# Handing the norm's reciprocal roots to all partitions through DRAM instead of TensorE, with every queue reordered

## What is computed

```python
q = softmax(Wq @ layernorm(x), over the 64 rows of a head) * SCALE
k = softmax(Wk @ ctx, over positions);  v = Wv @ ctx
out = Wo @ (per head: (k v^T)^T q) + bo                  # 128 x 1024 per batch
norm = max(sqrt(sum(out * out over the 128 channels)), 1e-12)
x = x + tanh(g_xattn) * out / norm * g * sqrt(128)
gate, up = bitlinear(layernorm(x), w_gate), bitlinear(layernorm(x), w_up)   # 2752 wide
x = x + tanh(g_ffn) * bitlinear(gate * up, w_down)
```

## Time and profile before

| | us |
|---|---|
| median of 3 runs (lowest, highest) | 1388.72 (1384.52, 1388.87) |
| span of the profiled execution, first to last instruction | 1386.2 |
| PE busy in it | 1314.9 (95%) |
| DVE busy | 1003.7 (72%) |
| ACT busy | 634.1 (46%) |
| POOL busy | 580.5 (42%) |

### The profile page before, as it was taken

One profiled execution on the slowest core, in us unless ns is written; L12 is line 12 of the kernel. 1 busy time (PEld: TensorE's weight loads), 2 busy tenths in 40 slices (PEclk: granted clock), 3 DMA queues, 4 the chain that ended last, 5 costly groups with the idle time before them and its releaser, 6 DMA issues. The chain is left out here.

```text
span 1386.2 us, 30208 instructions
## 1 busy us (share of the span) xinstructions
PE 1314.9 (95%) x12408; PEld 961.9 (69%) x12408; DVE 1003.7 (72%) x1343; ACT 634.1 (46%) x879; POOL 580.5 (42%) x357
## 2 busy tenths in 40 slices
PE   4787599999999899999999999999999999999999
PEld 2454387855787558876598757885598748985994
DVE  6977778878799976887688875889578866641330
ACT  4668786853544424453434533453344443320220
POOL 0249925866274472444334451346034432240120
PEclk8998799999999999999999999999999999999999
DMA  9939999896664879778777975787677895663421
GB/s 352 408 145 336 267 288 306 243 184 151 146 163 99 174 180 244 182 181 186 168 176 174 196 187 136 200 169 186 150 184 181 179 171 130 159 173 88 138 76 46
DMA packets 401417, 260.00 MB, mean 188 GB/s; under 512 B 325312, under 2 KB 342080, under 8 KB 401280
## 3 DMA queue, kind: packets, MB, share of 16 engines
q1 hardware_dynamic: 394368, 232.90, 67.3%
q10 hardware_dynamic: 6912, 25.17, 5.7%
HBM read 152.37 MB, written 25.95 MB: 129 GB/s over the span
## 5 line engine op out<-in xcount | busy, mean ns | idle before, releaser
L1118 PE MATMUL ps<-w_dn,inter_buf 128*128 128x512 fp8e4 x1376 | 307.8, 380 | 2.0 <-DVE inter_buf L1372 1.3
L1118 PEld LDWEIGHTS ps<-w_dn,inter_buf 128*128 128x128 f16 x1376 | 134.9, 99 | 157.8 <-issue 4.7
L1804 POOL TENSOR_TENSOR qs<-qs,q_stat 128x1024 f32<-128x1024 f32 x64 | 129.6, 2024 | 232.9 <-DVE q_stat L1615 232.9
L1034 PE MATMUL ps<-zT,w_gu 128*128 128x256 f16 x1664 | 191.2, 274 | 3.0 <-DVE zT L1372 2.4
L1034 PEld LDWEIGHTS ps<-zT,w_gu 128*128 128x128 fp8e4 x1664 | 163.0, 99 | 29.2 <-DVE zT L1372 2.6
L1069 PE MATMUL ps<-w_gu 128*128 128x128 f16 x2880 | 174.0, 219 | 2.7 <-DVE w_gu L1715 1.8
L1069 PEld LDWEIGHTS ps<-w_gu 128*128 128x128 fp8e4 x2880 | 165.8, 98 | 7.1 <-issue 3.1
L1860 POOL TENSOR_TENSOR w_gu<-w_gu 128x512 f32<-128x512 f32 x60 | 82.4, 1373 | 179.8 <-DVE w_gu L1715 112.6
L1069 PE MATMUL ps<-zT,w_gu 128*128 128x128 f16 x2176 | 132.6, 219 | 0.0
L1715 DVE SCALAR_TENSOR_TENSOR w_gu<-ps,w_gu 128x512 f32<-128x512 f32 x120 | 82.5, 688 | 68.0 <-PE ps L1069 67.9
L1069 PEld LDWEIGHTS ps<-zT,w_gu 128*128 128x128 fp8e4 x2176 | 125.5, 98 | 3.9
(11 more groups left out here) (195 smaller groups left out, 2588.8 us busy)
## 6 DMA issues: line engine op xcount, KB each, us to landing
w_gu<-forms SPq DMA_DIRECT2D x158, 256.0 KB, 3.0
ct_raw<-forms SPq DMA_DIRECT2D x52, 256.0 KB, 3.1
w_dn<-in_down_w SPq DMA_DIRECT2D x19, 512.0 KB, 6.0
xb<-in_x ACTq DMA_DIRECT2D x16, 512.0 KB, 6.8
x_dram<-xb SPq DMA_DIRECT2D x16, 512.0 KB, 3.9
fin<-x_dram SPq DMA_DIRECT2D x32, 256.0 KB, 2.9
out<-fin SPq DMA_DIRECT2D x32, 256.0 KB, 2.4
inter_buf<-in_up_w SPq DMA_DIRECT2D x15, 512.0 KB, 9.7
```

Source lines behind the costliest of these rows:

```text
L1034: last = nc.tensor.matmul(ps[:, rest_bank(g, j), s * T:s * T + T], w_gu[:, w, k, :], zT[:, h, k, :], start=(k == 0 and h == 0), stop=(k == ...
L1118: mm = nc.tensor.matmul(ps[:, down_bank(g, k), :], inter_of(g, j, u % 2, b), w_dn[:, j, hf * 512:hf * 512 + 512], start=(u == 0), stop=(u ...
L1804: nc.gpsimd.tensor_tensor(v, v, q_stat[:, u % 2, 1, :].unsqueeze(2).broadcast_to([P, 2 * HEADS, DH]), ALU.mult).then_inc(q_prob, 1)
```

## The change

`R` goes. SP gets two steps instead: `put_r` stores the 128 by 4 values of `rsv` to 2 KB of DRAM as 512 pieces of 4 bytes, and `get_r` loads these 2 KB back once for each of the 128 partitions, into `sq`, whose square is no longer needed by then. `x2m` reads `sq` and waits for that load. Bank OUT is free for the next `outp` after `ssg`, no longer after `x2m`. `rs` waits for the store of two halves earlier, since `rsv` has two buffers. All numbers of `WHEN` are new (of the table a line or two is shown).

```diff
     "rs": (2, 0, B), 
-    "R": (2, 0, B),
+    "put_r": (2, 0, B), "get_r": (2, 0, B),
...
+    "put_r": [164, 248, 349, 411, 673, 778, 935, 989, 1091, 1155, 1333, ...],
+    "get_r": [196, 303, 374, 421, 692, 794, 972, 991, 1125, 1163, 1353, ...],
...
+    r_dram = nc.dram_tensor("r_dram", [2 * B, 512], F32, kind="Internal").ap()
...
+            def put_r(i, hf):
+                wait(sp, rs_ready, 2 * i + hf + 1)
+                sp.dma_start(r_dram[2 * i + hf, :].rearrange("(k p) -> p k", p=P),
+                             rsv[:, hf, :], allow_slow_non_contiguous=True).then_inc(r_stored, 16)
+
+            def get_r(i, hf):
+                wait(sp, r_stored, 16 * (2 * i + hf + 1))
+                sp.dma_start(sq, r_dram[2 * i + hf:2 * i + hf + 1, :].broadcast_to([P, 512])).then_inc(r_in, 16)
...
-            def R(i, hf):
-                wait(pe, rs_ready, 2 * i + hf + 1)
-                wait_banks(out_free)
-                for k in range(4):
-                    last = nc.tensor.transpose(ps[:, OUT, k * P:k * P + P],
-                                               rsv[:, hf, k:k + 1].broadcast_to([P, P]), ident[:, :])
-                last.then_inc(r_ready, 1)
-                out_free[0] = (y_scaled, 2 * i + hf + 1)
...
             def x2m(i, hf):
-                wait(dve, r_ready, 2 * i + hf + 1)
+                wait(dve, r_in, 16 * (2 * i + hf + 1))
                 wait(dve, y_ready, 2 * i + hf + 1)
...
-                nc.vector.scalar_tensor_tensor(out=y, in0=ps[:, OUT, :], scalar=small[:, COEF_X:COEF_X + 1],
+                nc.vector.scalar_tensor_tensor(out=y, in0=sq, scalar=small[:, COEF_X:COEF_X + 1],
...
             def rs(i, hf):
                 wait(pool, ss_guarded, 2 * i + hf + 1)
-                wait(pool, r_ready, 2 * i + hf - 1)
+                wait(pool, r_stored, 16 * (2 * i + hf - 1))
```

More of the change, by code:

```diff
@@ L79 @@
     "e_f": (4, 0, BY_PE), "qf_hi": (4, BY_PE, B), "qf_lo": (4, BY_PE, B), "turn_q": (4, BY_PE, B),
-    "outp": (8, 0, B), "yev": (2, 0, B), "ss": (2, 0, B), "ssg": (2, 0, B), "rs": (2, 0, B), "R": (2, 0, B),
+    "outp": (8, 0, B), "yev": (2, 0, B), "ss": (2, 0, B), "ssg": (2, 0, B), "rs": (2, 0, B),
+    "put_r": (2, 0, B), "get_r": (2, 0, B),
     "ld_xr": (1, 0, B), "x2m": (2, 0, B), "x2a": (2, 0, B), "st_x2": (1, 0, B), "ln2": (1, 0, B),
@@ new lines @@
+    "outp": [175, 176, 177, 182, 250, 251, 252, 257, 322, 324, 325, 353, 390, 400, 401, 402, 637, 638, 639, 640,
[6 rows of a table added]
+    "yev": [190, 255, 368, 399, 669, 759, 924, 963, 1081, 1131, 1327, 1386, 1520, 1634, 1736, 1797, 1930, 1977,
[3 rows of a table added]
+    "ssg": [183, 274, 356, 410, 677, 777, 921, 971, 1079, 1158, 1345, 1396, 1543, 1636, 1761, 1824, 1954, 1992,
[3 rows of a table added]
+    "ld_xr": [0, 147, 592, 614, 1097, 1124, 1546, 1587, 1969, 1984, 2371, 2478, 2810, 2864, 3244, 3363],
[9 rows of a table added]
+    "zt_hi": [367, 464],
+    "zt_lo": [359, 475],
+    "z_hi": [865, 1038, 1378, 1456, 1806, 1863, 2057, 2301, 2671, 2727, 2908, 3170, 3452, 3507],
@@ new lines @@
+    "st_out": [978, 1008, 1088, 1417, 1471, 1472, 1522, 1660, 1859, 1915, 2022, 2026, 2332, 2333, 2524, 2577, 2739,
+        2756, 2886, 2887, 3189, 3190, 3234, 3333, 3521, 3536, 3570, 3603, 3700, 3706, 3713, 3715],
+    "lmax": [21, 22, 23],
+    "lsum": [47, 48, 54],
+    "lscale": [44, 45, 49],
+    "l_hi": [33, 43, 132],
+    "l_lo": [56, 206, 246],
+    "wpart": [211, 212, 671],
+    "wtotal": [225, 241, 661],
+    "wscale": [223, 228, 689],
+    "consts": [5],
+    "prod": [20],
+    "gains": [30],
@@ L331 @@
+    "get_r": [196, 303, 374, 421, 692, 794, 972, 991, 1125, 1163, 1353, 1425, 1577, 1640, 1773, 1821, 1958, 1990,
+        2163, 2262, 2372, 2427, 2607, 2666, 2807, 2836, 3075, 3103, 3221, 3297, 3421, 3481],
 }
@@ L800, in _ @@
                      "turn_k": turn_k, "turn_q": turn_q, "turn_z": turn_z, "turn_zs": turn_zs, "store_form": store_form,
-                     "load_form": load_form, "st_x2": st_x2, "reload": reload,
+                     "load_form": load_form, "put_r": put_r, "get_r": get_r, "st_x2": st_x2, "reload": reload,
                      "st_out": st_out})
@@ L1123, in _ @@
             program({"prod": prod, "lsum": lsum, "csum": csum, "msum": msum, "kt": kt, "qt": qt, "tr": tr,
-                     "mprod": mprod, "ctxk": ctxk, "ktr": ktr, "zt": zt, "wtotal": wtotal, "outp": outp, "ss": ss, "R": R,
+                     "mprod": mprod, "ctxk": ctxk, "ktr": ktr, "zt": zt, "wtotal": wtotal, "outp": outp, "ss": ss,
                      "gu": gu, "product": product, "down": down})
```

266 lines of the change are left out of this document (114 added, 152 removed), and 199 rows, old and new, of the table WHEN.

## The result

| kernel | runs | median us | lowest to highest |
|---|---|---|---|
| before | 4 | 1386.9 | 1384.5 to 1388.9 |
| changed | 4 | 1649.5 | 1641.8 to 1674.9 |

The ratio is 1.187 (95% interval 1.184 to 1.191): 263 us slower. Forecast were 1380, 1370 to 1393. The page of the changed kernel, span 1648.8 us: its first lines and slices, and the start of its last chain.

A forecast was written before the change was run, and what follows sets the result against it. TensorE was taken to bound the time behind 175 us, the chain to the first gu before it. Terms -12.3 - 1.3 + 3 + 2 = -8.6 gave a span of 1377.6, plus 2.5 around it: 1380 us, range 1370 to 1393.

The forecast's parts named there:

- What bounds the kernel now: Whole kernel: behind 175 us TensorE's work sets the time; ahead, the chain to the first gu at 173.1 us.
- The transposes removed: TensorE: 28 R of batches 2 to 15, 0.44 us each, save 12.3 us; the four in front count as nothing.
- Six matmuls moved: Front: batch 3's first kt goes ahead of the first gu, into a PE wait for zT, saving 1.3 us.
- The store and the load added: DMA trip of rsv through DRAM: store 2.9 us, load 2.9, bounds 2.0 each to 9.1 for a DMA.
- What the round trip is added to: Halves behind 175 us: values in SBUF 7.1 us behind ss; late x2m steps cost 3 us, bounds 0 and 7.
- The chain to the first gu: Front, batch 1: trip about even with slack, SP's later turn_k delays gu 2 us, bounds -2 and +12.
- The store of small pieces is slow: Rival, every trip: store lands X us later than forecast, making the kernel slower from X of about 4; chance 0.12.
- X = 6: Store landing 6 us later than forecast: 19 us lost behind 175 us, 10 in front, 1409 us in all.
- More than the transposes: Rival, whole kernel: no wait added, some old waits go, gu 2 us earlier; -16 as the middle, 1372 us; chance 0.13.
- The front pays it back: Rival, 140 to 175 us: small transfers behind weight loads make gu 10 us later, 1388 us; chance 0.18.

The follow-up runs named there:

- e_notrip: The changed kernel with neither store nor load, its order kept, x2m multiplying by the squares in the tile and waiting for rs alone; 1396.4 us.
- e_getonly: The changed kernel without the store, its load replaced by one of the same size from a row of x that waits for rs alone; 1391.9 us.
- e_quick16: The changed kernel storing 128 pieces of 16 bytes, with ScalarE writing the squares in turned order; 1418.0, 1418.6 and 1431.5 us, ratio 1.026.
- o_notrip: The kernel before, in its old order, without the transposes R and with nothing in their place; 1383.6 us, ratio 0.997.

## Why the prediction was wrong

*"What bounds the kernel now"* was right: two regimes, and in the second a wait of PE is paid in full. It left out the clock: with PE idle for 211 us behind 175 us, in many short waits, the mean granted clock there was 0.93 instead of 1.00, and with 128 matmuls fewer in the whole kernel PE was busy 60 us longer.

*"The transposes removed"*: 12.3 us, measured 4 (2 to 6 by the interval). PE's busy time behind 175 us fell by 10.3, not 12.3, and 4.3 us came back as idle time, nearly all of it in the one wait for nothing that shows. The four in front were worth nothing, as said.

*The new order* had no price in the sum but for the six matmuls. With the transposes and these gone and nothing added, the sum gives 1386.2 - 12.3 - 1.3 + 2.5 = 1375.1; e_notrip took 1396.4 and e_getonly 1391.9.

*"Six matmuls moved"* was not tried by itself.

*"The store and the load added"* is the step that failed. The load was priced at 2.9 and takes 3.0 alone and 4.5 to 4.9 in the kernels, a fair miss. The store was priced at 2.9: 2.0 of a store of 128 KB, and 0.9 for its pieces from the *loads* of 4-byte pieces, and that is the wrong row: loading the 512 pieces takes 2.1 us, storing them 7.2 to 11.2. In the changed kernel SyncE had it back after 8.5 at the least and 10.1 in the median. 2.0 to 9.1 was given as its bounds and a value near the low end taken; the upper one was nearly the truth. And the sum has no term at all for what the store does to other transfers and to SyncE's queue. The prediction had noted that only loads had a row and gave this a chance of 0.12.

*"What the round trip is added to"*: with the quick trip, 9.6 us from `rs` rather than 6.8, e_quick16 loses 27 us over e_getonly in the profiled run, where the sum had 3 us of waits and 2 in front, 7 and 12 at most. So the forecast would have failed with a quick store too. The sum counted only halves whose `x2m` makes PE late, each by its own excess in a schedule that otherwise kept its times. `x2m`, `x2a`, the next `yev` and the next `outp` follow each other, so a late one can pass on what it is late by; that this is where the rest went was not separated.

*"The chain to the first gu"*: 2 us later was forecast, within 171 to 185; measured were 2.3 earlier (170.8) with the quick store and 30 later (202.9) with the slow one. That the first lies so near is luck: the new order by itself brings `gu` 4 to 9 us earlier, which the sum did not have, and the quick trip then costs 7, which it held to be about even.

*The rivals.* "The store of small pieces is slow" was the right mechanism on the right side, and its price was wrong by a factor of nine. At X = 6 it gave 29 us over the forecast; the store was 5.6 us slower than said at the least and 7.2 in the median, and the time was 270 over the forecast. Of it 176 are not in the rival's sum at all: it let the slow store delay its own data, and never asked what else the DMA engines could do meanwhile. 32 stores of 8.5 us are 272 us in which other transfers are late. "More than the transposes" and "The front pays it back" did not come about.

Left open: why sixteen pieces in 64 B are so much worse than eight; how the 77 us split between SyncE's queue and the chain of `x2m`; what the new order loses by itself; what the one wait in o_notrip is; and whether an order made for the quick trip of 9.6 us would reach o_notrip's time.

## What to carry to other kernels

A DMA is priced by a row of its own direction and its own pattern of addresses, and where no row has both, its upper bound is the estimate to plan with. Beside "who waits for this transfer" stands the question whom it holds while it runs; the second cost more here than the first. A step that waits in a queue also holds what stands behind it: look at what was issued right after such a wait. And the time that an engine is spared is not yet time off the end: leave the work out with nothing in its place and look at that time before building a substitute.

## What the runs showed of the hardware

- A store to DRAM of adjacent 4-byte pieces from different partitions: 512 in 8.9 to 10.1 us, 128 in 7.2. The same 64 B apart: 2.0 and 1.5. As 128 pieces of 8, 16, 32 and 64 B: 2.9, 1.4 to 1.9, 1.4, 1.4.
- While such a store of 512 pieces is under way, a 256 KB load lands in 7.5 to 11.8 us on the same queue and in 6.1 to 8.2 on the other, instead of 2.5 to 2.8 alone.
- One row of 2 KB loaded to 128 partitions takes 3.0 us, a load of 256 KB of distinct rows 2.6.
- A 128x128 f32 weight load with elements four apart takes 327 ns instead of 198; a 128x512 Square whose neighbouring results go to columns 128 apart 1233 ns instead of 769.
- With PE idle 14% of the time behind 175 us in many short waits, the granted clock there was 0.93; with 1% idle it was 1.00.
